# Turning the negated row maximum of layer 0 through TensorE: one-column weights at partition 96 against full-size broadcast weights, and the rounding by a three-operand operation

## The reference

```
energy = einsum('nqhd,nkhd->nhqk', q, k)          # 16 heads of 8 features
energy = where(mask == 0, -1e20, energy)
attn   = softmax(energy * (1 / E ** 0.5), axis=3)
out    = einsum('nhqk,nkhd->nqhd', attn, v).reshape(N, Sq, E) @ Wo.T + bo
```

## Time and profile before

| | before |
|---|---|
| time, median of 3 runs | 1371.55 us (1370.35 to 1372.52) |
| the profiled execution's own time | 1371.72 us |
| its span, first to last instruction | 1370.0 us |
| PE busy | 1223.5 us (89%), 10408 instructions |
| DVE busy | 1026.2 us (75%) |
| ACT busy | 769.0 us (56%) |
| POOL busy | 395.0 us (29%) |
| mean granted TensorE clock | 0.972 |

### The profile page before, as it was taken

The page is one execution under the profiler, slowest core; times in us unless marked ns, Lnnn a source line. Parts: engine busy times, 40 slices in busy tenths (PEclk is TensorE's granted clock), DMA queues, the critical chain, the costliest instruction groups (busy, mean ns, idle before and its releaser), DMA issues.

```text
span 1370.0 us, 27816 instructions
## 1 busy us (share of the span) xinstructions
PE 1223.5 (89%) x10408; PEld 760.9 (56%) x10408; DVE 1026.2 (75%) x1662; ACT 769.0 (56%) x1013; POOL 395.0 (29%) x248
## 2 busy tenths in 40 slices
PE   0869899999999996788799999999999999999974
PEld 0335565566566566334356666656666666666642
DVE  6656666666666646877888888888888888888877
ACT  0525455555555555455666666666666666666642
POOL 6357666666566415332000000000000000000000
PEclk9979999999999997999999999999999999999996
DMA  5223244234333420010011110011110011110000
GB/s 151 76 78 79 80 114 113 77 101 110 96 90 104 116 58 18 0 46 0 8 38 46 46 44 22 25 45 45 45 45 20 26 44 45 45 45 23 1 0 14
DMA packets 29717, 74.66 MB, mean 54 GB/s; under 512 B 6384, under 2 KB 14960, under 8 KB 29664
## 3 DMA queue, kind: packets, MB, share of 16 engines
q1 hardware_dynamic: 23408, 70.78, 17.7%
q10 hardware_dynamic: 6256, 3.16, 0.9%
HBM read 42.30 MB, written 0.46 MB: 31 GB/s over the span
## 4 chain that ended last, share of the span: by engine, by line
PE 69%; DVE 13%; issue 8%; ACT 7%; ACTq 3%; POOL 0%; DVEq 0%
PE bank L826 13%; PE bank L808 13%; PE bank L768 8%; PE bank L684 7%; PE bank L708 5%; PE bank L712 5%; PE bank L725 4%; DVE bank_max L1497 3%; ACTq L416 2%; DVE region L1639 2%; PE bank L849 2%; ACT region L1141 2%; PE bank L797 2%; DVE e_row L1458 2%; PE bank L1053 2%
## 5 line engine op out<-in xcount | busy, mean ns | idle before, releaser
L1458 DVE CUSTOM_DVE_ANT_0 e_row<-bank,region 112x1500 f32<-112x1500 f32 x128 | 220.1, 1720 | 129.4 <-PE bank L684 128.4
L1176 ACT CAST region<-bank 125x768 f16<-125x768 f32 x224 | 178.7, 798 | 206.2 <-PE bank L768 206.2
L1141 ACT ACTIVATE region<-bank 125x896 f32<-125x896 f32 x192 | 176.0, 917 | 210.0 <-PE bank L712 209.9
L808 PE MATMUL bank<-region 128*128 128x500 f16 x1008 | 234.6, 378 | 14.7 <-ACT e_row L1167 13.3
L1516 DVE TENSOR_TENSOR region<-bank,region 125x768 f16<-125x768 f32 x224 | 209.7, 954 | 25.4 <-ACT region L1176 25.4
L1497 DVE TENSOR_REDUCE bank_max<-bank 128x1 f32<-128x500 f32 x336 | 208.8, 671 | 10.6 <-PE bank L808 10.6
L514 POOL TENSOR_TENSOR region<-c_in,region 125x1536 f16<-125x1536 f32 x16 | 49.7, 3108 | 560.8 <-ACT region L1191 560.8
L768 PEld LDWEIGHTS bank<-ident,e_row 128*125 128x125 f32 x1344 | 175.5, 188 | 31.2 <-DVE region L1516 5.5
L768 PE MATMUL bank<-ident,e_row 128*125 128x128 f32 x1344 | 179.5, 273 | 3.3 <-DVE region L1516 2.6
L1167 ACT ACTIVATE e_row<-bank,neg_max 128x1500 f32<-128x1500 f32 x112 | 169.7, 1515 | 20.2 <-DVE neg_max L1501 20.0
L808 PEld LDWEIGHTS bank<-region 128*128 (+1 forms) x1008 | 93.3, 98 | 115.6 <-issue 11.4
(11 more groups left out here) (212 smaller groups left out, 1471.0 us busy)
## 6 DMA issues: line engine op xcount, KB each, us to landing
c_in<-in_ctx SPq DMA_DIRECT2D x32, 750.0 KB
region<-region SPq DMA_DIRECT2D x64, 192.0 KB, 2.7
region<-in_mask_Bx1xSxS_if SPq DMA_DIRECT2D x32, 328.1 KB
region<-region SPq DMA_DIRECT2D x64, 96.0 KB, 2.5
region<-region SPq DMA_DIRECT2D x8, 750.0 KB
g_w<-region SPq DMA_DIRECT2D x8, 750.0 KB
g_w<-in_L_ffn_rt_gate ACTq DMA_DIRECT2D x1, 1024.0 KB, 9.9
u_w<-in_L_ffn_rt_up ACTq DMA_DIRECT2D x1, 1024.0 KB, 17.4
```

Of the source, the lines that this page charges most:

```text
L808: last = pe.matmul(bank[:, k, 0:4 * KP], q1[:, ql, b, 128 * t:128 * (t + 1)], c_t1[par][:, cl, 4 * k:4 * k + 4, 0:KP], start=(ql == 0 and ...
L1141: act.activation(p0[:, 2 * i:2 * i + 2, :], ring0("s", h, i)[0:KP, :, 0:HALF_ROWS], ACT.Exp, scale=SCALE0)\
L1176: act.copy(p_high1[grp][:, UC * u:UC * (u + 1), 128 * at:128 * (at + 1)], pair_chunks(unit_no(1, par, ("turn", t, u)), 128)).then_inc(sem( ...
L1458: dve.tensor_tensor_reduce(out=masked.rearrange("p (a k) -> p a k", a=3), in0=bank[0:R0, 0:3, 0:4 * KP], in1=mask_bias[par][:].rearrange(" ...
```

## The change

The weights of the four turning matmuls become 112 by 128, the same column repeated, and the output takes all 128 partitions of PSUM in place of partition 96 alone; L1473 still reads partition 96. `none_valid` gets 112 rows in place of 56, and its matmul 112 by 128 weights in place of 56 by 125. On DVE both small operations become `scalar_tensor_tensor`, whose third operand is a tensor in SBUF: `ones_f` for `none_valid`, and a new constant `unfold` for `negc`. One DVE memset fills `unfold` at the start, and DVE waits once for it before its first maximum.

```diff
+        unfold = sb("unfold", [128, 4])
-        none_valid = sb("none_valid", [S, 1], F16)
+        none_valid = sb("none_valid", [R0, 1], F16)
...
             for t in range(4):
-                last = pe.matmul(place[96:97, 0, R0 * t:R0 * (t + 1)], negc[:, t:t + 1], ident16[0:R0, 0:R0],
+                last = pe.matmul(place[:, 0, R0 * t:R0 * (t + 1)], negc[:, t:t + 1].broadcast_to((R0, 128)), ident16[0:R0, 0:R0],
                                  start=True, stop=True)
             if h == 0:
-                last = pe.matmul(place[0:KP, 1, 0:S], none_valid[:].broadcast_to((S, KP)), ident16[0:S, 0:S],
+                last = pe.matmul(place[:, 1, 0:S], none_valid[:].broadcast_to((R0, 128)), ident16[0:R0, 0:S],
                                  start=True, stop=True)
...
             if h == 0:
-                dve.tensor_scalar(none_valid[:], neg_max[0:S, 0:1], MASKED, None, ALU.is_ge)
-            dve.tensor_scalar(negc[:], neg_max[0:R0, 4 * h:4 * h + 4], FOLD_MAX * FOLD, 1.0 / FOLD, ALU.min, ALU.mult)\
+                dve.scalar_tensor_tensor(none_valid[:], neg_max[0:R0, 0:1], MASKED, ones_f[0:R0, 0:1], ALU.is_ge, ALU.mult)
+            dve.scalar_tensor_tensor(negc[:], neg_max[0:R0, 4 * h:4 * h + 4], FOLD_MAX * FOLD, unfold[0:R0, :], ALU.min, ALU.mult)\
                 .then_inc(sem("negc0"), 1)
...
+            dve.memset(unfold[:], 1.0 / FOLD).then_inc(sem("fold_const"), 1)
...
+            dve.wait_ge(sem("fold_const"), 3)
             for t in range(4):
                 dve_max0(dve, 0, 0, t)
```

## The result

The changed kernel takes 1363.13 us as the median of 6 runs (1362.63 to 1367.69), the kernel before 1371.25 us beside it (6 runs). The ratio is 0.9944, with a 95% interval of 0.993 to 0.9959. The execution that was profiled is the slowest of the six, 1367.69 us with a span of 1365.9, so its profile has to be read part by part.

A forecast was written before the change was run, and what follows sets the result against it. PE was taken to bound the kernel, with the turn on its chain in both halves. PE's 5.0 us gained less 0.9 lost, net 4.1, and zero on DVE took the median 1371.55 to 1367.5 us; range 1365.0 to 1375.0.

The forecast's parts named there:

- The steps between tile sizes: On PE at the turn, each change between narrow or low and full tiles costs about 0.1 us; three per first half, two per second.
- Nothing gained on PE: Rival, chance 0.10: the 0.1 us steps aren't of tile size, or savings become waiting for DVE; time within 1.5 us of 1371.5.
- the dependence on a semaphore: Part of the no-gain rival on PE: the 0.1 us steps at the turn come from the semaphore, not the tile's size.
- DVE: The two small operations ahead of the turn: no difference in duration, between -0.6 and +2.2 us, and the wait for POOL unchanged.
- The stalls: DVE's waits for POOL at `negc`, 4.95 us once, 1.12 and 1.32, were to stay, as the new operation is held too.
- the sign for `negc`: What would show the forecast: the new `negc` operation still takes about 5 us once, 1.1 to 1.3 twice, 0.25 in steady second halves.
- Lost turn: Rival, chance 0.16: in batch 2 POOL's next instruction comes between `none_valid` and `negc`, +6.6 us, 1374.1 us.
- wide loads in series: Rival, chance 0.06: each broadcast load at PE's turn takes its recorded 128 ns unhidden, +5.9 us, 1377.5 us.
- not held: Rival, chance 0.08: the new DVE operation escapes POOL, three stalls of 6.9 us go, and low clock behind the longest; 1356.9 us.
- The first load: PE's first turning load, grown from 1 to 128 columns, is exposed behind `negc`: 0.028 us per turn, 0.9 us lost in all.
- the first step: The tile-size step ahead of the turning matmuls, 0.09 us, left out of PE's gain because PE was said to wait for `negc`.
- the PE term: PE's sum at the turns: 5.0 us gained, 0.9 lost, net 4.1 us, bounds 2.7 and 7.9 us.

The follow-up runs named there:

- e5_negc_wide: Against the kernel before, only `negc`'s four turning weights made full-size, `none_valid`'s matmul left narrow, both small DVE operations `tensor_scalar`; 1370.67 us, ratio 0.9994.
- e6_none_wide: Against the kernel before, only `none_valid`'s matmul made full-size, `negc`'s weights left at one column, both small DVE operations `tensor_scalar`; 1367.95 us, ratio 0.9983.
- e7_w125: Against the kernel before, all turning weights of 125 columns writing 125 partitions, both small DVE operations `tensor_scalar`; 1368.29 us, ratio 0.9978.
- e3_dve_only: Against the kernel before, only DVE's half of the change: both small operations `scalar_tensor_tensor`, with the old matmuls; 1370.64 us, ratio 0.9997.
- e4_odd: Full-size weights as in the change, but `none_valid` by `tensor_scalar` and `negc` by two `tensor_scalar` of 3 and 1 columns; 1370.4 us, ratio 0.9994 to the kernel before.
- e10_again2: The changed kernel unaltered, run once more for another profile, of an execution of 1363.27 us; median 1363.63 us, ratio 0.9946 to the kernel before.
- e1_again: The changed kernel run again with nothing changed, for a second profile; 1365.44 us, ratio 0.9947 to the kernel before.
- e2_pe_only: Against the kernel before, only PE's half of the change: full-size weights, both small DVE operations still `tensor_scalar`; 1366.44 us, ratio 0.9963.

## Why the prediction was right, and where it was wrong

**The steps between tile sizes: right, with their size.** I had read 0.1 us for each step off the chain and said that three of them in a first half and two in a second would go. The chain after reads 0.64 and 0.66 for the scores (0.64 to 0.66 were named) and 0.03 for `none_valid` (0.05). `e5_negc_wide` and `e6_none_wide` show the steps behind the narrow matmuls, and `e7_w125` shows that full-size tiles are enough for them, without 128 columns. In every other second half the step behind the turn doesn't come back, which I had in all: the scores keep 0.75, and from the start of L693's piece to the end of the scores it is 1.02 us in the changed kernel (0.27 and 0.75), in `e5_negc_wide` (0.27 and 0.75) and in `e7_w125` (0.33 and 0.69), against 1.05 before. So something else sets the time there, and no run shows what. "Nothing gained on PE" is refuted, and so is the dependence on a semaphore: the waits are the same in all of these.

**DVE: right.** The stalls stay as foreseen, and `e3_dve_only` puts the new operations at nothing. Only the sign for `negc` was named wrongly: since `none_valid` takes the long wait, `negc` has no instance of 5 us (at most 1.29). Their own 12 to 14 ns lie within the bounds, between -0.02 and +0.07 us.

**Lost turn, wide loads in series, not held: none came.** POOL started behind both small operations. Four loads of 98 ns pass in 0.26 us, 0.065 each.

**The step that failed: "The first load. It can't be hidden, as it waits for `negc`", with "Of these 0.29 us I leave out the first step (0.09), since PE waits there for `negc` in any case".** PE doesn't wait there. The chain of before already passed straight through PE at this place: the load starts at 262.66, and the piece of L692 only at 262.73, where the matmuls ahead end. I read the load's start against the end of `negc` without setting it beside the end of the matmuls ahead. In the changed kernel the load starts at 246.12 and the last L713 ends at 246.24 in the chain; in the timeline:

```profile
245.91 0.15 DVE L1471 SCALAR_TENSOR_TENSOR negc<-neg_max,unfold 112x4 f16<-112x4 f32 x1
246.12 0.21 PEld L693 LDWEIGHTS bank<-ident,negc 112*128 112x128 f16 x4
```

A load of 0.098 us fits into these 0.12. So it costs nothing, and the group of four, with the step in front of it, gains. The load starts 0.05 us behind the end of `negc` (259.43 against 259.38) where it started 0.09 behind it in the earlier trace rows. I had the group of four, with its start, losing 0.038 us in each half (0.01 for the pace and 0.028 exposed). In the chain it gains 0.03. That is 0.07 in each half, 0.14 in a batch. The load is hidden by little. In `e4_odd` `negc` comes some 0.06 us later, so that the load starts only 0.06 ahead of the piece's start, in place of 0.12, and the group takes 0.31 in place of 0.26 (load, then chain):

```profile
245.32 0.21 PEld L693 LDWEIGHTS bank<-ident,negc 112*128 112x128 f16 x4 [0.19 <-DVE negc L1472]
```

```profile
245.38 0.31 PE bank L693 x4
```

Against the 0.14 stands the second half in two that gains 0.03 in place of 0.13. In the chain two batches lose 2 x 0.26 + 0.13 + 0.03 = 0.68 us, and between the copies 0.71, or 0.355 each. For 16 batches this is 5.7 us in place of 4.1. My upper bound of 7.9 us for the PE term had this case in it ("if PE gets the first step back as well"), but the range began at 1365.0. By itself this step leaves the time at 1371.55 - 5.7 = 1365.9, still inside the range. What carried it below is a term that the forecast's sum put at nothing without a reason, the clock: about 1.3 us in batch 2 and, between the two profiles near their medians, 1.4 at the start.

The Trainium skill has a rule for the loads that I passed over. "TensorE: Matmul & The Clock Gate", section "Weight-path perf modes — Fast Weight Load (FWL) and DoubleRow", has a faster load come on by itself when the number of weights is 128 and the type isn't FP32. The traces agree: 98 ns with 128 columns, 135 with 125, both float16. The rule of the Trainium skill that the prediction named, in the same page's section "LDWEIGHTS (loading the stationary operand)", would give 107 and 104 ns for these two, an estimate from the page. It differs from the measurement, above all for 125 columns, and has the wrong sign between them.

**The term that the sum lacked: the clock, here around the stall of batch 2.** The two intervals of batch 2 fell by 1.7 us in `e10_again2`, not by the steady 0.36. The windows of the 3 us from 144 on say why, first of before, then of the changed kernel (`after`), then of `e3_dve_only` and `e6_none_wide`:

```profile
144.00:147.00 3.00, 3.00 (x30) 2.44 (x32) 0.66 (x2) 1.21 (x2) 3.00 (x1) 0.50 0.00 0
```

```profile
144.00:147.00 3.00, 3.00 (x39) 2.16 (x38) 0.38 (x1) 2.36 (x2) 2.82 (x1) 0.91 0.00 0
```

```profile
144.00:147.00 3.00, 3.00 (x33) 2.13 (x32) 0.00 (x0) 1.98 (x2) 2.88 (x1) 0.50 0.00 0
```

```profile
144.00:147.00 3.00, 3.00 (x50) 2.08 (x51) 0.97 (x1) 2.54 (x3) 2.32 (x1) 1.00 0.00 0
```

PE has the stall behind it and is busy all the time in each. With the narrow `none_valid` matmul (before, `e3_dve_only`, `e5_negc_wide`) it is still at 1.2 GHz, and stays there until more than 6 us behind the copy; with the wide one (the other seven profiles that have the stall) it is back at 2.4 GHz 3 to 4 us behind it. Some 2 to 3 us fewer at half speed are worth about 1.3.

PE doesn't recover faster for that. Summed over windows of 1 us, the stretch at 1.2 GHz is 6.8 us long in nine of the ten profiles, narrow or wide. What differs is where it begins. In the three narrow ones that is 0.2 to 0.7 us ahead of the copy, in six of the wide ones 2.8 to 3.8 us ahead, inside the stall, where PE stands idle and a low clock costs nothing. These are two microseconds of the stall, of before and of `after`:

```profile
138.00:140.00 2.00, 0.00 (x0) 0.00 (x0) 2.00 (x1) 0.00 (x0) 2.00 (x1) 1.00 0.31 132
```

```profile
138.00:140.00 2.00, 0.02 (x1) 0.05 (x2) 1.83 (x2) 0.00 (x0) 2.00 (x1) 0.50 0.31 129
```

The seventh wide one, `e6_none_wide`, begins 0.4 us ahead of the copy, and its stretch is only 3.4 us long. In the six the clock fell before the wide matmul of this turn had run, so its width there isn't what moved it. Narrow and wide kernels divide without exception in these ten profiles, but no run shows why.

So the 6.5 us of layer 0 (6.4, 6.5 and 6.6 in `e1_again`, `e2_pe_only` and `e10_again2`) are 5.7 from the turns and 1.3 from batch 2's clock, less about 0.5 in the first and last halves, where PE waits for others. In `after` itself it is 5.6, since one late interval has 13.17 us where the others have 12.28.

**What stays open.** The medians fell by 8.1 us, 1.6 more than layer 0. Over all 15 runs of the changed kernel the mean is 1364.1 and over all 61 of the kernel before 1371.5, so that the means differ by 7.4 only. The rest goes with where stretches at 1.2 GHz fall at the start and behind layer 0. Between the profile before and `e10_again2`, both near their medians, the spans differ by 8.4 us: 6.6 are layer 0, and 1.4 the start, where 12.7 us at 1.2 GHz ahead of the first copy stand against 9.4. These stretches differ between executions and between nearly equal kernels: `e2_pe_only` has the same layer 0 and a median 3 us higher, and `e4_odd` loses its whole gain there. Whether the change itself made the shorter start more frequent isn't shown. No run was made that holds the stretches still, and what decides them isn't known. A forecast of this kernel to better than some 2 us needs them.

## What to carry to other kernels

A small matmul among full-size ones cost 0.10 us of PE at the change of size behind it, however few columns it had, and its own group 0.03 us more than the full-size one. So make its weights 128 columns (125 took 0.06 us more for four) and its output full height, and make all neighbours so, since one narrow one keeps the steps around it. Then look at every instance of the turn and not at two: in every other second half most of the gain stayed away. Before a load is called exposed or hidden, set its start beside the end of the matmul ahead of it in the same chain; the end of what it waited for says nothing by itself. And compare the stretches at 1.2 GHz of the two profiles before a difference is put down to the edit: those behind layer 0 took back between nothing and all of what was won in it.

## What the runs showed of the hardware that wasn't expected

- A broadcast load of 128 float16 columns takes 98 ns (`after`) and one of 125 columns 135 (`e7_w125`), both over 112 partitions. The load of 1 column takes 82 (L692 before).
- The change from a narrow to a full-size tile costs 0.10 us (0.74 against 0.64 for the scores, 0.13 against 0.03 for L696), and one narrow matmul keeps the steps of its neighbours too.
- A three-operand DVE operation of 1 element with two SBUF inputs is let in 0.4 us ahead of the recorded end of POOL's `tensor_scalar` (done at 139.76 against 140.20). A `tensor_scalar` of 3 or 4 elements is held until its end (4.95 us), and one of 1 element beside the same instruction isn't (0.15 us).
- The stretch at 1.2 GHz that the stall of batch 2 brings is 6.8 us long in nine of ten profiles, but begins up to 3.6 us earlier or later against the end of the stall. What it costs depends on how much of it falls into the stall: 3 to 4 us of it or more than 6 lie behind the copy.
